# Edge pass of a graph layer: on the vector engine, the differences of the softmax chain behind the weighing of the values instead of in front of it

## The reference

```
xn  = layernorm(x)
# graph part: attention over the incoming edges of every node, 4 heads of 64
xg  = xn + mean of edge-type embeddings per source node
q, k, v = xg @ Wq + bq, xg @ Wk + bk, xg @ Wv + bv
alpha = sum(q[dst] * k[src], per head) / 8
a     = exp(alpha - segment_max(alpha, dst)[dst])
out   = segment_sum(a * v[src], dst) / segment_sum(a, dst) + xg @ Ws + bs
# mixing part on xn: an attention over features, layernorm, 256 -> 768 -> 256 with gelu
# then x = x + out + mix, and a dense layer of 8 experts with softmax weights on layernorm(x)
```

## Time and profile before

| what | value |
|---|---|
| median of 3 runs | 2811.33 us (2808.03 to 2815.71) |
| profiled execution, its own time | 2796.99 us |
| its span in the trace | 2795.3 us |
| TensorE busy, of the span | 2449.1 us (88%) |
| VectorE busy | 2143.5 us (77%) |
| ScalarE busy | 1389.7 us (50%) |
| GpSimd busy | 923.9 us (33%) |

### The profile page before, as it was taken

The page is one execution under the profiler, slowest core; times in us unless marked ns, Lnnn a source line. Parts: engine busy times, 40 slices in busy tenths (PEclk is TensorE's granted clock), DMA queues, the critical chain, the costliest instruction groups (busy, mean ns, idle before and its releaser), DMA issues.

```text
span 2795.3 us, 42254 instructions
## 1 busy us (share of the span) xinstructions
PE 2449.1 (88%) x13352; PEld 2052.7 (73%) x13352; DVE 2143.5 (77%) x3905; ACT 1389.7 (50%) x2619; POOL 923.9 (33%) x891
## 2 busy tenths in 40 slices
PE   6478994799899889899888988867999999999998
PEld 4267773677677677777767777646988888888898
DVE  6797552898998989989898999857666666666665
ACT  5421110465566555656655656545555555555554
POOL 0140004566666666656656666600000000000000
PEclk9799997999999999999999999988999999999999
DMA  5131456566666666666666666630000000000000
GB/s 155 28 115 39 141 175 192 168 194 196 194 201 192 197 185 197 204 186 195 199 192 183 197 198 192 185 123 16 14 16 16 16 16 16 16 16 14 14 9 12
DMA packets 189689, 336.31 MB, mean 120 GB/s; under 512 B 31112, under 2 KB 128688, under 8 KB 189446
## 3 DMA queue, kind: packets, MB, share of 16 engines
q0 software_dynamic: 67104, 219.09, 26.1%
q1 hardware_dynamic: 122374, 114.53, 13.6%
HBM read 293.84 MB, written 40.48 MB: 120 GB/s over the span
## 4 chain that ended last, share of the span: by engine, by line
PE 70%; DVE 18%; issue 7%; another core or an unknown queue 2%; DVEq 1%; ACT 1%; DMA 0%; SPq 0%; POOL 0%; ACTq 0%; POOLq 0%
PE ps L1390 19%; PE ps L1286 11%; PE ps L1400 10%; PE ps L1275 8%; PE ps L1151 5%; PE ps L1253 3%; PE ps L1246 3%; DVE ring L1738 3%; DVE ring L1791 2%; DVE rows L1487 2%; PE ps L1064 2%; PE ps L1231 1%; DVE nodes L1805 1%; PE ps L1071 1%
## 5 line engine op out<-in xcount | busy, mean ns | idle before, releaser
L811 POOL DMA_INDIRECT ring<-kv_rows,idx x832 | 870.8, 1047 | 764.6 <-issue 261.8
L1390 PE MATMUL ps<-f_split,e_up 128*128 128x512 f32 (+1 forms) x1664 | 501.8, 383 | 7.2 <-DVE e_low L1952 6.8
L1275 PE MATMUL ps<-nodes,ohT 128*128 x1664 | 418.2, 396 | 96.8 <-issue 50.1
L1275 PEld LDWEIGHTS ps<-nodes,ohT 128*128 128x128 f32 x1664 | 321.0, 198 | 171.2 <-issue 124.4
L1286 PE MATMUL ps<-ring 128*128 128x260 f32 x1664 | 445.7, 414 | 0.0
L1928 DVE TENSOR_TENSOR f_split<-f_more,f_split 128x1024 fp32r<-128x1024 f32 (+1 forms) x208 | 242.0, 1164 | 237.0 <-ACT f_split L996 233.4
L990 ACT ACTIVATE f_more<-ps,e_rest 128x512 f32<-128x512 f32 (+1 forms) x416 | 289.1, 746 | 268.1 <-PE ps L1390 267.4
L1286 PEld LDWEIGHTS ps<-ring 128*128 128x128 f32 x1664 | 316.4, 200 | 43.4
L1390 PEld LDWEIGHTS ps<-f_split,e_up 128*128 128x128 f32 x1664 | 305.7, 190 | 55.4 <-DVE e_low L1952 7.5
L923 ACT ACTIVATE nodes<-ps 128x780 f32 x208 | 170.7, 820 | 296.0 <-PE ps L1286 265.1
L1390 PE MATMUL ps<-f_split,e_low 128*128 128x512 f32 (+1 forms) x832 | 315.3, 379 | 0.0
(11 more groups left out here) (348 smaller groups left out, 3477.7 us busy)
## 6 DMA issues: line engine op xcount, KB each, us to landing
relq<-rel_rows SPq DMA_DIRECT2D x208, 128.0 KB
ring<-kv_rows,idx POOLq DMA_INDIRECT x832
kv_rows<-work SPq DMA_DIRECT2D x49, 256.0 KB, 2.2
xn_rows<-nodes SPq DMA_DIRECT2D x1, 6272.0 KB, 22.3
sx_rows<-work SPq DMA_DIRECT2D x49, 128.0 KB, 1.7
nodes<-in_x_dram SPq DMA_DIRECT2D x4, 1536.0 KB
work<-in_x_dram SPq DMA_DIRECT2D x48, 128.0 KB, 2.3
m_xn<-xn_rows SPq DMA_DIRECT2D x24, 256.0 KB
```

Source lines behind the costliest of these rows:

```text
L811: pool.indirect_dma_start(out=kvh(c)[:, g, 0:2 * D], out_offset=None, in_=kvD, in_offset=bass.IndirectOffsetOnAxis(ap=idx[c // KP][:, s:s ...
L1275: last = pe.matmul(ps[:, 2048 + D * g:2048 + D * (g + 1)], ohT[c % 2][:, g * P:(g + 1) * P], nodes[:, ds(win[g] * AC + HG * AC, D)], start ...
L1390: last = pe.matmul(bank(2 * l + m, 0, n * P), e_parts[l][w][:, e, i, m * P:(m + 1) * P], src_[a][:, i * QW:i * QW + n * P], start=(i == 0 ...
```

## The change

In the vector engine's `step`, the block that weighs the values of slots `i-7` is moved in front of the block that waits for the sums and computes the differences. Nothing is added or removed.

```
                 ch = lambda d: (c - d) % U // CH
+                if not known or 0 <= i - LAG < NHF:
+                    if (c - LAG) % CH == 0:
+                        dve.wait_ge(sem("a_made"), k(LAG) + 1)
+                    weigh(i - LAG, (c - LAG) % U)
                 if c % CH == 2 and (not known or i >= 6 and i - 6 < NHF):
                     sums_seen(i)
                     go, _ = chained("schain", k(6) * 10 + 5)
                     differences(k(6), ch(6) % 2, go)
-                if not known or 0 <= i - LAG < NHF:
-                    if (c - LAG) % CH == 0:
-                        dve.wait_ge(sem("a_made"), k(LAG) + 1)
-                    weigh(i - LAG, (c - LAG) % U)
                 if not known or i - LAG - 1 >= 0:
                     go, _ = chained("schain", k(LAG + 1) * 10 + 8)
                     add_up(i - (LAG + 1), (c - LAG - 1) % U, go)
```

## The result

| | before | after |
|---|---|---|
| median of 6 runs each, us | 2810.12 (2808.03 to 2816.01) | 2828.45 (2822.08 to 2836.14) |
| ratio | | 1.0067 [1.0044, 1.0091] |
| profiled execution, us | 2796.99 | 2823.96 |

The account below looks back on a forecast made before the run. Handovers, not a saturated engine, were taken to bound the edge pass. The terms 10.4 - 6.0 - 0.9 + 0.3 - 1.2 - 0.9 gave +1.7 us, taken as +0.7: 2811.3 to about 2812 us, range 2805 to 2819.

Parts of the forecast that it names:

- The register load, 0.62 us per piece-3 step: Piece-3 steps without a wait: add_up's load stands bare behind L1782, L1327 0.62 us later; 17 steps, +10.4 us.
- The six with a wait of 0.75 us: Six piece-3 steps where L1779 waits about 0.75 us: L1805 ends 0.25 us earlier, -1.2 us together.
- Piece-7 steps, -6.0 us: Piece-7 steps with the full 1.25 us wait at L1779: L1327 0.38 us earlier in 16 steps, -6.0 us.
- rival 1: Slower: piece-3 steps pay, L1327 in piece-7 steps can't move forward; +8.6 us, about 2820 us; chance 0.17.
- I count a shift of L1327 one to one, in both directions: Edge pass: any delay or advance of TensorE's L1327 stays and counts in full.
- Waits of L1738 for something outside: VectorE's products wait 22.9 us in 7 places; these can take in a delay, up to 1.3 us off.
- Rival 2, load hidden, -13: Faster: L1805 follows L1782 at once, piece-3 steps without a wait cost nothing; about -13 us, 2798 us; chance 0.13.
- Rival 3, VectorE the bound: Much faster: idle time before L1779 that a weighing can fill goes, 36 to 39 us, 2773 us; chance 0.04.
- From L1327 of a piece-3 step to the next still 25.8: Edge pass after the change: interval from a piece-3 step's L1327 to the next L1327 stays 25.8 us.

Follow-up runs that it names:

- e16: Changed kernel with the register load ahead of the weighing, and plain transfers in place of the indirect gathers: 2733.91 us.
- e14: Changed kernel with plain transfers in place of the indirect gathers: 2747.03 us.
- e13: Kernel before with plain transfers of the same size in place of the indirect gathers: 2730.21 us.
- e15: Kernel before with the weighing first in piece-3 steps alone, and plain transfers in place of the gathers: 2746.73 us.
- e17: Kernel before with add_up directly behind the differences, its register load ahead of them, and plain transfers in place of the gathers: 2730.68 us.
- e4: Kernel before with six chained memsets between the register load and add_up in piece-3 steps: 2831.42 us, ratio 1.0094.
- e8: Kernel before with two TensorE signals (fc1_ps of piece 5, x1_ps of piece 0) given by later matmuls: 2784.35 us, ratio 1.0198.
- set 2789: Set of runs in which the kernel before had a median of 2789 us; the changed kernel, run once more there, measured ratio 1.0041.
- e1: Kernel before with the weighing first in piece-7 steps alone, with gathers: 2824.87 us, ratio 1.0053.
- e2: Kernel before with the weighing first in piece-3 steps alone, with gathers: 2806.09 us, ratio 1.0002.
- e6: Kernel before with three more semaphore increments on GpSimd ahead of the gather issues: 2729.26 us, ratio 0.9999.
- set 2729: Set of runs in which the kernel before had a median of 2729 us.

## Why the prediction was wrong

- *The register load, 0.62 us per piece-3 step:* right. 0.54 us "issue" ahead of L1805 and L1327 at 3.70 are in the trace; e16 shows that this load is nearly the whole cost (16.8 without it 3.7). The number of steps was short: +10.4 - 1.2 for 17 and six steps stood against 25 of one kind in e14. The six with a wait of 0.75 us were steps with late sums: L1779 starts 1.4 to 1.6 us behind the end of L1286 there, and in no such step of e13 does it wait that long. The counts of the prediction also make only 50 of its 51 steps.
- *Piece-7 steps, -6.0 us:* the step that failed. I read 0.30 us of idle TensorE as room for L1327. In the changed kernel TensorE comes to L1220 0.36 us later, and without late signals (e13) L1805 has 0.77 us of slack. The wait of 1.25 us for the sums, from which the term was built, is 0.61 there; the rest was a late signal. The term is worth nothing: e15, with the piece-3 steps alone, measured the same as e14. The chance that I gave rival 1 (0.17) named this; its range to 2825 and its +8.6 had the cost of only 17 steps. With 25 steps of 0.64 us and no gain the sum would have been +16.
- *"I count a shift of L1327 one to one, in both directions":* half wrong. The delay stays, but because VectorE carries it to L1738 and L1275, not because of L1327. The advance does not (e17). The earlier trace rows showed a delay alone. And with late signals about, a delay of 1.78 us did not stay in full (e4).
- *"Waits of L1738 for something outside", up to -1.3:* misread. These were late signals of L1275; e13 has no such wait.
- *Rival 2, load hidden, -13:* e16 answers it: with the load out of the way +3.7 against e13 of another set, and the same intervals. The cost goes, but no gain comes.
- *Rival 3, VectorE the bound:* wrong as a gain, but VectorE is the bound from the scores of a piece-3 step to the next products, which is why 0.54 us of its idle time costs the whole amount.
- *"From L1327 of a piece-3 step to the next still 25.8":* 25.85 here and 25.23 without late signals, in both orders.

What remains open is how the 18 us of the first set divide into the 16 us of the piece-3 steps, more late signals (138 for 106, 21 gelus for 10) and what shorter waits for late sums gave back. e8 shows that late signals cost time, but no run splits this sum. That 18 lies so near to 16.8 is in part chance: the same change cost 12.5 us in set 2789.

## What to carry to other kernels

An operation put in front of a wait fills it, but what it had covered (here a register load of 0.3 us with its sequencer work) is bare afterwards, and that costs in full where its engine is the bound (0.64 us per step in e14). Idle time of 0.3 us in front of a handover is a gain only if the other engines of that stretch have room, so look at both neighbouring intervals, and test an advance by itself. If a wait's releaser is "remote", or the rows of one kernel have two sizes for the same wait, compare parts of a change on a version without that disturbance; their times on a disturbed one may mislead, as the parts in e1 and e2 did.

## What the runs showed of the hardware

- The same kernel took 2729 to 2810 us in different sets, and 2729 and 2792 in two sets for which the record lists the same chip. The difference lies in the edge pass: from the first to the last L1738 1394.7 us in the profile before and 1332.3 in e6, while the stretches ahead of it and behind it differ by under 7 us each. The traces differ in the waits for "remote": none in set 2729, 10 for the gelu alone in the profile before.
- A consumer saw the end of a matmul group usually 0.04 us behind its row's end, and in other executions of the same instruction 1.4 to 5.3 us behind it (L906 and L1701, kernels before and after). In the five runs with plain transfers in place of indirect gathers this did not happen.
- VectorE's register load takes 0.30 us, and 0.54 us pass between the operation ahead of it and the one behind it when nothing covers it (changed kernel and e14). It started 0.013 to 0.017 us behind the start of L1782 in all 51 steps, before and after, so not while L1782 still waited.
